# Edge pass of a graph network: column marks moved into the PSUM bank of the turned weights

## What is computed

```python
hs, hd = h[src], h[dst]
a = sum(hs * hd, axis=-1)                          # score of an edge
g = sigmoid(...)                                   # three gates of an edge, [E, 3]
alpha = seg_softmax(a, dst)                        # over the edges of a target node
beta = seg_softmax(g, dst)
h_att = segment_sum(alpha[:, None] * (hs @ node_att_W summed), dst) / 3
h_rel = segment_sum(einsum('em,emf->ef', beta, hs @ rel_att_W[m]), dst) / 3
```

## Time and profile before

| | us |
|---|---|
| median of 3 runs | 2215.26 |
| lowest and highest of them | 2212.79, 2216.94 |
| the profiled execution, its time | 2217.47 |
| the profiled execution, its span from first to last instruction | 2215.7 |

### The profile page before, as it was taken

How to read it: one execution, slowest core, us unless ns; L and a number is a source line. 1 busy time by engine, 2 the same in 40 slices (tenths; PEclk the granted TensorE clock), 3 DMA queues, 4 the chain that set the end, 5 groups by cost and what they waited for, 6 DMA issues and landing times. The chain is left out here.

```text
span 2215.7 us, 43419 instructions
## 1 busy us (share of the span) xinstructions
PE 1641.7 (74%) x9963; PEld 1000.0 (45%) x9963; DVE 1319.9 (60%) x5221; ACT 1128.0 (51%) x3319; POOL 1612.1 (73%) x1703
## 2 busy tenths in 40 slices
PE   5877777787788888944877677766777676777774
PEld 5222222222233323213646566655666565665664
DVE  4765566556554554444766666666666666665669
ACT  3434343333444444621666666555656566655548
POOL 5767777777777777777677777777777777777635
PEclk8989999999899999975989989899888999889888
DMA  8453444343434434435522222222222222222213
GB/s 277 160 184 128 130 130 130 128 150 115 145 130 136 133 122 149 151 110 113 181 67 66 66 66 66 62 65 66 61 66 65 66 60 66 66 62 65 62 57 119
DMA packets 115985, 235.06 MB, mean 106 GB/s; under 512 B 32910, under 2 KB 68231, under 8 KB 106423
## 3 DMA queue, kind: packets, MB, share of 16 engines
q0 software_dynamic: 52832, 109.39, 20.4%
q1 hardware_dynamic: 56522, 97.21, 12.0%
q10 hardware_dynamic: 6540, 27.42, 3.5%
HBM read 166.01 MB, written 67.89 MB: 106 GB/s over the span
## 5 line engine op out<-in xcount | busy, mean ns | idle before, releaser
L461 POOL DMA_INDIRECT d_region<-d_h,d_region x784 | 755.8, 964 | 248.0 <-issue 209.5
L214 POOL DMA_INDIRECT acc<-d_src_product,b_region x760 | 718.4, 945 | 251.8 <-issue 200.6
L907 DVE SCALAR_TENSOR_TENSOR banks<-banks,b_region,acc 128x128 f32<-128x128 f32 x784 | 277.1, 354 | 419.2 <-DMA acc<-d_src_product,b_region 418.6
L1683 DVE TENSOR_TENSOR acc<-acc,banks 128x160 f32 x784 | 252.3, 322 | 220.4 <-PE banks L1482 84.4
L689 PE MATMUL banks<-acc,b_region 64*128 64x512 f32 x1176 | 318.9, 649 | 35.9 <-ACT acc L795 18.4
L1448 PE MATMUL banks<-shift_ident,d_region 128*128 128x128 f32 x784 | 135.1, 297 | 249.6 <-DMA d_region<-d_h,d_region 237.9
L917 DVE SCALAR_TENSOR_TENSOR acc<-acc,b_region,banks 128x128 f32<-128x128 f32 x784 | 264.3, 337 | 0.0
L1479 PE MATMUL banks<-d_region 128*128 128x128 f32 x1568 | 247.9, 310 | 0.2 <-DVE d_region L1644 0.2
L1482 PE MATMUL banks<-d_region,pick 128*128 128x128 f32 x1568 | 241.4, 303 | 0.0
L1479 PEld LDWEIGHTS banks<-d_region 128*128 128x128 f32 x1568 | 233.4, 227 | 1.3 <-issue 0.4
L795 ACT ACTIVATE gate_col<-banks,b_region 128x1024 f32<-128x1024 f32 x147 | 158.5, 1111 | 142.0 <-PE banks L689 140.9
(11 more groups left out here) (271 smaller groups left out, 2428.3 us busy)
## 6 DMA issues: line engine op xcount, KB each, us to landing
d_runs<-acc SPq DMA_DIRECT2D x48, 1024.0 KB, 4.4
acc<-ea ACTq DMA_DIRECT2D x25, 1024.0 KB, 5.2
d_region<-d_h,d_region POOLq DMA_INDIRECT x784
d_region<-d_rel SPq DMA_DIRECT2D x49, 256.0 KB
acc<-d_src_product,b_region POOLq DMA_INDIRECT x760
hT<-xT SPq DMA_DIRECT2D x7, 448.0 KB, 7.4
d_src_product<-acc SPq DMA_DIRECT2D x7, 448.0 KB, 7.1
d_gates<-acc ACTq DMA_DIRECT2D x196, 6.0 KB
```

The source lines that it names most:

```text
L214: pool.indirect_dma_start(self.rows[:, s, j, :], None, table, bass.IndirectOffsetOnAxis(self.idx[:, k:k + 1], 0)).then_inc(self.gathered[s ...
L461: pool.indirect_dma_start(rows[:, s, :], None, table, bass.IndirectOffsetOnAxis(idx[:, s:s + 1], 0)).then_inc(gathered[q], 16)
L907: nc.vector.scalar_tensor_tensor(stepped[:, k % STEPS, :], wwp, wgt[:, k:k + 1], rows[:, s, j, :], ALU.mult, ALU.add).then_inc(ch, 1)
L1683: nc.vector.tensor_tensor(w, w, UZ[q % 2][:, :, j, :], ALU.add).then_inc(ad, 1)
```

## The change

The marks `oh` move from SBUF to columns 256 to 383 of PSUM bank 2, the bank into whose columns 0 to 127 TensorE turns the weights. The row 0, 1, ..., 31 with which `one_hot` compares is copied once, ahead of the loop, to columns 128 to 159 of the same bank, and read from there. As TensorE and VectorE now both use that bank, two waits are added: the turn of group q waits for the gate weights of group q, and the gate weights of group q wait for the turn of group q-1. No instruction leaves the loop and none is added to it but the waits.

```diff
-def one_hot(nc, t, table, col, out):
+def one_hot(nc, iota_w, table, col, out):
 
     rel = table[:, bass.ds(col, GJ)].unsqueeze(2).to_broadcast([P, GJ, W])
-    return nc.vector.tensor_tensor(out, t["iota_w"][:, :].unsqueeze(1).to_broadcast([P, GJ, W]), rel, ALU.is_equal)
+    return nc.vector.tensor_tensor(out, iota_w.unsqueeze(1).to_broadcast([P, GJ, W]), rel, ALU.is_equal)
...
-        oh = ca(GJ * W).rearrange("p (j w) -> p j w", j=GJ)
...
+        iota_p = WEIGHTS[:, P:P + W]
+        oh = WEIGHTS[:, 2 * P:3 * P].rearrange("p (j w) -> p j w", j=GJ)
...
             def turn_weights(it, q):
                 pe.wait_ge(ex, it * NG + (q + 1 + CREDIT))
                 pe.wait_ge(wt, it * NG + (q - 1 + 1 + CREDIT))
+                pe.wait_ge(bw, it * NG + (q + 1 + CREDIT))
                 nc.tensor.transpose(WEIGHTS[:, 0:P], PT[q % 2], ident[:, :]).then_inc(pt, 1)
...
             dve.wait_ge(gsd, 2 * M + 1)
+            c.link(nc.vector.tensor_copy(iota_p, t["iota_w"][:, :]))
...
                 dve.wait_ge(ug, it * NG + (q - 2 + 1 + CREDIT))
                 dve.wait_ge(bw, it * NG + (q - 1 + 1 + CREDIT))
-                one_hot(nc, t, t["rel_col"], col, oh).then_inc(ohs, 1)
+                dve.wait_ge(pt, it * NG + (q - 1 + 1 + CREDIT))
+                one_hot(nc, iota_p, t["rel_col"], col, oh).then_inc(ohs, 1)
                 dve.wait_ge(ohs, it * NG + (q + 1))
```

## The result

The changed kernel takes 2610.5 us (median of 4 runs, 2606.4 to 2613.9) against 2216.1 us: ratio 1.177, 95% interval 1.175 to 1.180. The profiled execution took 2613.5 us, 396 us more than the one of before.

The account below looks back on a forecast made before the run. POOL's gathers bound the kernel at about 5.02 us a step; the new wait closes a 6.76 us ring (3.57 + 3.19), so 1.3 + 195 x (6.76 - 5.024) = 340 us more: 2555 us, range 2340 to 2650.

Parts of the forecast that it names:

- the ring: Edge pass: turn, sums, add_windows, lowest, marks and product wait on each other, one group per turn; 6.76 us a step.
- The part of the ring outside turn and sums: VectorE's path from the sums' end through add_windows, lowest and product to the next turn: 3.57 us.
- Turn and sums: TensorE's weight turn through the end of the sums: 3.19 us with clock falls, 2.10 at full level.
- The 0.48 us taken off: Saving on 3.67 us sums: 1.1 us of turn and sums run at full level before the clock falls.
- The upper end: Rival with TensorE at half clock through every sum, 3.71 us: ring 7.28 us, 2654 us; no separate chance given.
- The clock as the large term: TensorE's 2.4 us stand before each turn makes its clock fall behind most stands, lengthening the sums.
- the rival with the clock held: Ring binds at full clock, 5.67 us a step: 2342 us; chance 0.24 with rings up to 6.2 us.
- Two instructions at PSUM: VectorE's marks and product using PSUM: 300 ns and an unchanged 560 ns, no PSUM surcharge counted.
- VectorE's added wait: Marks' wait for the earlier turn is met before add_windows could have started: costs nothing.
- The first turn and the tail: Edge pass ends: first turn waits 1.3 us for the first product; tail behind the last turn unchanged.
- The signs to look for: Edge pass: turn step 6.8 us, TensorE stand 2.4, gathered-row wait nearly nothing, POOL idle 0.75, clock 0.7 or 0.8.
- The faster rival: POOL stays the bound and gathers lose VectorE's product disturbance: at most 20 us saved, 2196 us; chance 0.03.

Follow-up runs that it names:

- e1_waits_only: Kernel before plus only the two added waits, marks and index row left in SBUF: 2607.8 us, ratio 1.176.
- e2_psum_no_waits: Kernel before with marks and index row in the PSUM banks only the sums write, without the added waits: 2202.6 us, ratio 0.9933.
- e4_turn_last: Changed kernel with sums(q) issued ahead of turn_weights(q+1) on TensorE, both waits kept: 2212.1 us, ratio 0.9978 to the kernel before.
- e3_fill8: Changed kernel plus eight unread 128x128 matmuls per group on TensorE ahead of the turn: 2363.1 us, ratio 1.066 to the kernel before.
- e6_dve_wait_only: Kernel before plus only VectorE's added wait, marks in SBUF: 2222.0 us, ratio 1.001.
- e7_before_fill8: Kernel before plus eight unread 128x128 matmuls per group ahead of the turn: 2219.6 us, ratio 1.0002.
- e5_marks_first: Kernel before plus the two added waits, with marks and product issued ahead of lowest and picks on VectorE: 2570.2 us, ratio 1.159.

## Why the prediction was right, point by point

The forecast was 2555 us in a range of 2340 to 2650; 2610.5 lies in it.

- **Who closes the ring.** Right, and shown from both sides: e1_waits_only has the whole loss without PSUM, e2_psum_no_waits PSUM without the loss, and e4_turn_last opens the ring with everything else in place.
- **The part of the ring outside turn and sums.** Forecast 0.25 + 0.20 + 1.77 + 1.35 = 3.57 us. Measured, means of 180 steps: 0.15 + 0.20 + 1.83 + 1.42 = 3.60. The handover was 0.10 us too long, because it was read from a sum and not from a turn. The two VectorE stretches were 0.13 too short, because the two neighbouring steps they were read from held no loop edge and no late penalty. That the sum fits to 0.03 us is luck in part: the two misses cancel.
- **Turn and sums.** The mis-sized term: 3.19 us forecast, 3.45 measured (median 3.66). 195 x 0.26 = 51 us, the most of the 55 missed. Where the clock falls was wrong: the forecast let it fall 1.1 us behind the start of the turn. In the changed kernel 102 of the 196 turns run at half from their start (0.44 us, as at 1599.77 us; the median of L1473 is 444 ns, 307 before), and with them turn and sums take 3.91 us on average. With the 94 turns that start at the full level they take 2.99.
- **The 0.48 us taken off.** This was reckoned wrongly. What TensorE does in 1.1 us at the full level takes 1.1 x 3.71/2.10 = 1.94 us at half, so by the forecast's own premise the saving is 0.84 us, the term 2.83, the ring 6.40 and the time 2485 us, still in the range. That 2555 came nearer than this is luck: the saving was reckoned too small, and the fall came earlier than taken, which asked for a smaller one.
- **The upper end.** The 3.71 us taken for "wholly at half" hold a turn at the full level (0.30 us). With the 4.00 us of the step at 1599.77 us the ring's upper end is 7.57 us, that is 2713 us, and the range stopped short of it.
- **The clock as the large term.** Right: e3_fill8 gives 2363 us where the rival with the clock held was put at 2342, so the fork between the two was real, and the clock's share is 247 of the 394 us. Its mean step is 5.75 us against 5.67 forecast, through the same late steps on VectorE; that is 16 of the 21 us between the two.
- **Two instructions at PSUM.** Forecast 300 and 560 ns, measured 300 and 558. The 65 ns that the Trainium skill, "VectorE: DVE Perf Modes", in its section on the TRN2 errata gives a PSUM read more than an SBUF read did not show in either (294 ns before for the marks, 560 for the product); the measurement decides.
- **VectorE's added wait.** Forecast nothing; e6_dve_wait_only shows none.
- **The first turn and the tail.** The first turn came 4.0 us later, not 1.3; 2.8 of that lie ahead of the edge pass, whose first gather began that much later in this execution (1104.3 against 1101.5 us). The pass's tail was longer by 1.7 us and what follows the pass shorter by 2.4. None of it matters.
- **The signs to look for.** L1473's step 7.04 (6.8 forecast), TensorE's stand 2.04 us (2.4), the wait for gathered rows gone, POOL's idle 0.82 us (0.75), clock 0.70 (0.7 to 0.8), no gather over 961 ns in all 784. The stand came out shorter than forecast because TensorE's own path ahead of it also runs slower after a fall: the four matmuls of L1449 take up to 1.1 us at half and 0.6 at full.
- **The faster rival.** Its mechanism was real and its price near: 20 us forecast as the most, 15 measured in e2_psum_no_waits. Its condition was also put rightly; the placing of the marks, not their being in PSUM, decided.

## What to carry to other kernels

A wait that orders two engines is priced by what stands behind it in its engine's queue: draw the chain from the waiting step through that queue to the producer and see whether it comes back to the start one step later. If it does, add it up and compare it with the present step; if it does not, the wait may be long and cost nothing, as in e4_turn_last. Ahead of adding a wait for a shared bank, look for a bank whose two users are already ordered by a wait that exists.

A ring through TensorE with a stand in it can cost more than its length: here 247 of the 394 us came from the clock that fell with the stand. Matmuls that nobody reads, put into the stand, tell the two shares apart, as long as they end ahead of what the stand waits for (e3_fill8) and do not come near to being the bound themselves (as in e7_before_fill8).

## What was not expected of the hardware

- Eight fp32 matmuls of 128x128 appear as 16 records and take 2.03 us at the full level, 127 ns each.
- The length of the stand does not settle alone whether the clock falls. Stands of about 1.8 us let it fall in every step of e5_marks_first, whereas in the kernel before waits of 1.6 to 2.0 us were followed by long sums 30 times in 93. In e5_marks_first the granted clock (0.75 on average from 1500 to 2000 us) falls 176 times in the 176 steps between 1200 and 2400 us; why the steps settle at 6.5 to 6.8 us in that way stays open here.
- With the clock already down at the turn, turn and sums take 3.91 us on average in the changed kernel (100 steps), against 2.15 at the full level (e3_fill8).
